# A four-phase kernel: the gated product moves into PSUM, residual work moves between VectorE and GpSimd, and the last normalisation is shared out anew

## The chip, the cores and the metric

The kernel runs on one core of one Trainium2 chip. The metric is the device time of one execution, in microseconds (us). Three executions of the kernel before took 1301.18, 1302.83 and 1308.39 us; the median is 1302.83 us. The names of the engines in the profile are PE (TensorE matmuls), PEld (TensorE weight loads), DVE (VectorE), ACT (ScalarE), POOL (GpSimd) and SP (SyncE).

## The reference, cut to what matters

The input is x of shape (2, 2048, 128). Four blocks follow one another, each as x = x + layernorm(block(layernorm(x))): an RWKV-like time mix with its channel mix, a ternary-weight feed-forward, a state-space block and a mixture of 8 experts of which each token uses 2. The change touches the first and the last.

```python
# the time mix (L0_attn), per batch and channel
xxx = h + (h - x_shifted) * ts                     # h = layernorm of the block's input
k, v, r = xxx @ Wk.T, xxx @ Wv.T, sigmoid(xxx @ Wr.T)
wkv = scan over time: out = (e1 * aa + e2 * vv) / (e1 + e2), with the running maximum bb
x = x + r * wkv                                    # the residual that the change moves
# the mixture of experts (L1_ffn), top 2 of 8
h = silu(x @ w1[e]) * (x @ w3[e])                  # the gated product
out = sum over the 2 experts of  weight_e * (h @ w2[e])
# around it
x = x + (out - mean(out)) / sqrt(var(out) + eps)
```

## The kernel before, in words

Channels lie on the 128 partitions. The 2 x 2048 tokens are cut into NT = 4 tiles of N = 512 tokens for each of B = 2 batches. Each phase is a block with one instruction stream for each engine, written out by hand; engines meet only at semaphores, and a phase ends with a barrier of all engines. Nothing schedules the order: it is that of the code.

**The time mix** (`phase_time_mix`, lines 164 to 600). VectorE does most of it, tile by tile. For tile t and each batch b it runs `sums` (a scan over `fac`, line 520), `normalise` of tile t+1 (lines 471 and 474: `pC` in PSUM times `rstd` in SBUF), `shift_and_mix`, `distances` (line 528), `maxima`, `weigh_values`, `steps`, `ln2_scale` of tile t-1, `clip_steps`, `numerators` (a scan, line 544) and `blend` (lines 552, 556 and 559, each for both batches). `blend` ends with line 562, which copies the last column of two running rows to their first column by a multiplication and maximum over 4 elements. GpSimd then multiplies the blended value by the gate (line 439) and adds the residual (line 441), for batch 0 and then batch 1. `ln2_centre` on TensorE reads that sum, and ScalarE squares it (`ln2_square`). ScalarE's stream is in order: behind the squares of tile t-1 stand the exponentials of tile t, which `weigh_values` (line 539) needs.

**The mixture** (`phase_moe`, line 1857 and on). Routing sorts the token-expert pairs into TILES = 39 tiles of 256 rows, each for one expert. For each tile GpSimd issues two indirect DMAs that gather rows (line 2277) and two that scatter the results (line 2294). The first 8 tiles are gathered ahead; from then on GpSimd's stream is scatter tile i, gather tile i+8. TensorE turns the rows (`x_turn`), VectorE copies them out as 16-bit pairs (`take_x`, line 2504), and two units n of each tile follow: `up` (24 matmuls a tile at lines 2014 to 2016) writes the two products of a unit into the banks `R1` and `R3`; ScalarE takes silu of `R1` (line 2231); VectorE multiplies `R3` by it into `hid` in SBUF (line 2520); ScalarE rounds `hid` to 16 bits (`hid_high`, line 2217); VectorE writes the rest, `hid` less its rounded value (`hid_low_part`, line 2511); `down`, LAG = 3 units later, multiplies both by w2; ScalarE copies the result into one of 4 buffers `y` (line 2223), which GpSimd scatters.

**The end** (same function). The DMA queue of SP reads all results back, in 8 groups of 4 chunks of 128 tokens. For group i VectorE adds the two experts' rows and their sums (`add_up`, line 2535, with the sums in `sums`), and makes `minus`, the negated means (line 2540); ScalarE squares the deviations with their sums (`spread`, line 2245) and forms the inverse root; VectorE multiplies twice over 4 columns (`weigh`, `scale_of`); GpSimd scales the group (line 2307, four instructions of 128x128); TensorE turns it (line 2154); VectorE adds it to X (`add_out`, line 2556); SP stores it. `scaled` and the bank `R1` each have two buffers.

## Time and profile before

| what | value |
|---|---|
| three executions, median | 1302.83 us |
| the profiled execution's own time | 1301.92 us |
| its span in the trace | 1300.1 us |
| time mix, to its barrier | 0 to about 133 us |
| channel mix and feed-forward, state-space block | about 133 to 985 us |
| routing of the mixture | to about 1062 us |
| the 39 tiles of the mixture | about 1062 to 1264 us |
| read back, last normalisation, stores | to the end |

The profiled execution lies between the lowest and the median of the three. The busy time of an engine is the sum of its instructions' spans; matmuls overlap in the records, so a PE that is busy in all of a window need not be at its peak. In a timeline row the bracket is the idle time ahead of the instruction and what ended it; "issue" means that nothing the profile shows was waited for.

### The profile page before, as it was taken

What the parts mean: (1) busy time and instruction counts of PE and PEld (TensorE: products, weight loads), DVE (VectorE), ACT (ScalarE), POOL (GpSimd) and SP (SyncE); (2) the same over time, 40 slices, a digit from 0 to 9 for tenths busy, and PEclk for the clock granted to TensorE, in tenths of its full rate; (3) what the DMA queues carried; (4) which work ended last, traced back from release to release, by engine and by line L of the source; (5) the groups of instructions that cost most, each with busy time, mean ns of one, the idle gap of its engine ahead of it and who ended that gap; (6) DMA issues with size and microseconds to landing.
All of it is one profiled execution on the core that took longest, in us unless ns stands there. A gap on an engine that the chain in (4) does not pass through costs nothing. (4 is left out here: it accounts for less than half of the span.)

```text
span 1300.1 us, 16587 instructions
## 1 busy us (share of the span) xinstructions
PE 1073.6 (83%) x4914; PEld 543.4 (42%) x4914; DVE 985.6 (76%) x1333; ACT 731.6 (56%) x1163; POOL 738.3 (57%) x617
## 2 busy tenths in 40 slices
PE   6655669999999997979898898989797569988853
PEld 2211224444444442433333333434233459977753
DVE  6996776575664546999999999999993587765535
ACT  6773454555645446748575675766563336544434
POOL 0223342151421202899889889897985257777764
PEclk8885799999999997999999999999998569998986
DMA  6000000000000002323232322222220111111225
GB/s 228 1 1 0 0 1 1 1 2 1 0 0 0 1 0 82 102 69 109 71 98 72 100 89 90 74 72 70 70 73 1 65 30 51 49 50 51 49 50 193
DMA packets 32552, 67.07 MB, mean 52 GB/s; under 512 B 5760, under 2 KB 5952, under 8 KB 32256
## 3 DMA queue, kind: packets, MB, share of 16 engines
q1 hardware_dynamic: 27056, 55.16, 13.0%
q0 software_dynamic: 4992, 10.23, 2.9%
q8 instruction: 39, 0.64, 0.2%
q10 hardware_dynamic: 432, 0.76, 0.2%
q14 instruction: 33, 0.27, 0.1%
HBM read 56.57 MB, written 9.57 MB: 51 GB/s over the span
## 5 line engine op out<-in xcount | busy, mean ns | idle before, releaser
L1750 POOL TENSOR_TENSOR prod<-hs,csb 128x1024 f32<-128x1024 f32 x128 | 301.9, 2359 | 139.1 <-DVE hs L1797 138.5
L1797 DVE TENSOR_TENSOR_SCAN hs<-dA,carry,pD 128x512 f32<-128x512 f32 x256 | 313.8, 1267 | 5.2 <-DVE pD L1810 0.8
L1519 PE MATMUL pY<-prod,const 128*128 128x512 f32 x512 | 247.0, 606 | 1.8 <-POOL prod L1750 1.8
L1659 ACT ACTIVATE dA<-dt,negA 128x512 f32<-128x512 f32 x256 | 168.0, 713 | 17.3 <-POOL dt L1719 15.8
L1810 DVE TENSOR_TENSOR pD<-dtu,pD 128x1024 f32<-128x1024 f32 x128 | 155.3, 1214 | 7.5 <-PE pD L1533 7.4
L1519 PEld LDWEIGHTS pY<-prod,const 128*128 128x128 f32 x512 | 97.6, 194 | 119.3 <-issue 114.7
L2277 POOL DMA_INDIRECT g<-moe_rows,source x78 | 83.1, 1065 | 49.7 <-DVE source L2469 26.3
L2520 DVE SCALAR_TENSOR_TENSOR hid<-pR,silu 128x512 f32<-128x512 f32 x78 | 53.9, 691 | 63.1 <-ACT silu L2231 63.1
L1003 ACT ACTIVATE stage<-pR,vec 128x512 f32<-128x512 f32 x64 | 43.9, 687 | 100.2 <-PE pR L703 100.0
L2294 POOL DMA_INDIRECT moe_outs<-y,to x78 | 82.1, 1052 | 24.8 <-issue 22.8
L2014 PE MATMUL pR<-x,moe_hi 128*128 128x256 f16 x312 | 87.3, 280 | 2.2 <-DVE x L2504 2.2
L2015 PE MATMUL pR<-x,moe_hi 128*128 128x256 f16 x312 | 87.5, 280 | 0.0
L2016 PE MATMUL pR<-x,moe_lo 128*128 128x256 f16 x312 | 87.2, 279 | 0.0
L2231 ACT ACTIVATE silu<-pR 128x512 f32<-128x512 f32 x78 | 46.5, 596 | 59.6 <-PE pR L2016 58.7
L1053 POOL TENSOR_TENSOR z_lo<-z,z_hi 128x512 f16<-128x512 f32 x8 | 10.6, 1326 | 106.2 <-DVE z_hi L1140 106.2
L1448 PE MATMUL pQ<-xn,convw 128*128 128x512 f32 x112 | 58.4, 646 | 13.6 <-DVE xn L1780 13.6
L439 POOL TENSOR_TENSOR o<-o,rs 128x512 f32<-128x512 f32 x8 | 14.4, 1800 | 97.2 <-DVE o L559 97.2
L1533 PE MATMUL pD<-split,sel 96*128 96x512 bf16 x128 | 50.1, 392 | 19.3 <-DVE hs L1797 18.9
L1042 POOL TENSOR_TENSOR K_lo<-kstage,K_hi 128x512 f16<-128x512 f32 x24 | 28.8, 1203 | 53.7 <-DVE K_hi L1115 53.7
L2126 PE MATMUL pY<-moe_hi,hid_hi 128*128 x312 | 57.8, 223 | 0.8 <-DVE hid_lo L2511 0.8
L2128 PE MATMUL pY<-moe_hi,hid_lo 128*128 x312 | 57.8, 223 | 0.0
L2127 PE MATMUL pY<-moe_lo,hid_hi 128*128 x312 | 57.7, 223 | 0.0
(423 smaller groups left out, 2574.2 us busy)
## 6 DMA issues: line engine op xcount, KB each, us to landing
csb<-ssm_c SPq DMA_DIRECT2D x128, 256.0 KB, 3.1
raw<-moe_w SPq DMA_DIRECT2D x12, 512.0 KB, 4.9
room<-moe_outs SPq DMA_DIRECT2D x8, 512.0 KB, 8.0
hidw<-hid_w SPq DMA_DIRECT2D x1, 2048.0 KB, 9.9
moe_rows<-xt SPq DMA_DIRECT2D x8, 256.0 KB, 2.0
outT<-X SPq DMA_DIRECT2D x8, 256.0 KB, 2.0
X<-xT SPq DMA_DIRECT2D x3, 512.0 KB, 4.1
g<-moe_rows,source POOLq DMA_INDIRECT x78, 2.8
```

Source lines behind the costliest of these rows:

```text
L1448: last = nc.tensor.matmul(Q[c][:], convw[:, c, k, :], xn[b][:, k:k + N], start=k == 0, stop=k == TAPS - 1)
L1519: last = nc.tensor.matmul(YB[c][:], G.ident, prod[:, slot(b, n), c, :], start=n == 0, stop=n == DST - 1)
L1659: last = nc.scalar.activation(dA[:, slot(b, n), c, :], dt[:, b, c, :], ACT.Exp, scale=negA[:, c, n:n + 1])
L1750: nc.gpsimd.tensor_tensor(prod[:, slot(b, n), :, :], hs[:, slot(b, n), :, :], csb[:, slot(b, n), :, :].to_broadcast([P, CB, N]), ALU.mult)\
L1797: last = nc.vector.tensor_tensor_scan(hs[:, slot(b, n), c, :], dA[:, slot(b, n), c, :], dBu(n, c), carry[:, b, n, c:c + 1], ALU.mult, ALU.add)
L1810: nc.vector.tensor_tensor(DD[:, (n % 2) * CB:(n % 2) * CB + CB, :], dtu[:, b, :, :], bcastB(n).unsqueeze(1).to_broadcast([P, CB, N]), ALU. ...
L2014: nc.tensor.matmul(out, w_hi, x_hi, start=start, stop=False)
L2015: nc.tensor.matmul(out, w_hi, x_lo, start=False, stop=False)
L2016: return nc.tensor.matmul(out, w_lo, x_hi, start=False, stop=stop)
L2126: nc.tensor.matmul(out, hid_hi[:, n % HR, at], w_hi, start=u == 0 and h == 0 and r == 0, stop=False)
L2277: nc.gpsimd.indirect_dma_start(g[:, i % GR, r, :], None, rows, bass.IndirectOffsetOnAxis(ap=source[:, 2 * i + r:2 * i + r + 1], axis=0))\
L2294: nc.gpsimd.indirect_dma_start(outs, bass.IndirectOffsetOnAxis(ap=to[:, 2 * i + r:2 * i + r + 1], axis=0), y[:, i % YR, r, :], None).then_ ...
```

## The change

In the time mix VectorE takes over part of GpSimd's work. In `blend` of tiles 0 to 2 batch 1 goes first, and its gate product and residual sum are done by VectorE; GpSimd does only batch 0's two. In the last tile VectorE does all four. The copy of the carried columns at the end of `blend` is gone; `steps` carries the columns of the sums and numerators with those it carried already, and the last tile has a small copy of its own (`carry_numerators`). `normalise` of tile t+1 stands ahead of `sums` in every tile, and on ScalarE `inverse_roots` ahead of `step_exponentials`.

In the mixture `hid` in SBUF is gone. The product stays in the bank of `R3` from which it was read; `R3` has three banks in place of two, `XG` one in place of two, and the small uses of the second XG bank go to the third of `R3`. `up` of unit n waits for `hid_low` of unit n-3 and for silu of unit n-2, where it waited for the product of unit n-2.

At the end `spread` takes `sums` itself and scales by -128; the factor is taken out again in the logarithm's scale. `minus` is made by GpSimd. GpSimd scales groups 0 to 5; VectorE scales groups 6 and 7 (`scale_up`).

```diff
                 if t + 2 < NT:
                     square(t + 2)
+                    inverse_roots(t + 2)
                 if t + 1 < NT:
                     step_exponentials(t + 1)
-                if t + 2 < NT:
-                    inverse_roots(t + 2)
...
-            for t in range(NT):
-                for b in range(B):
-                    pool.wait_ge(S["shift"], at(t, b))
-                    pool.wait_ge(S["gate"], at(t, b))
-                    nc.gpsimd.tensor_tensor(o[:, b, :], o[:, b, :], rs[:, t % 2, b, :], ALU.mult).then_inc(S["gated"], 1)
-                    pool.wait_ge(S["gated"], at(t, b))
-                    nc.gpsimd.tensor_tensor(XA[:, b, ds(t)], o[:, b, :], xn[:, t % 3, b, :], ALU.add)\
-                      .then_inc(S["added"], 1)
+            for t in range(NT - 1):
+                pool.wait_ge(S["shift"], B * t + 2)
+                pool.wait_ge(S["gate"], at(t, 0))
+                nc.gpsimd.tensor_tensor(o[:, 0, :], o[:, 0, :], rs[:, t % 2, 0, :], ALU.mult).then_inc(S["gated0"], 1)
+                pool.wait_ge(S["gated0"], t + 1)
+                nc.gpsimd.tensor_tensor(XA[:, 0, ds(t)], o[:, 0, :], xn[:, t % 3, 0, :], ALU.add).then_inc(S["added0"], 1)
...
-                nc.vector.tensor_copy(run[:, :, 0:2, 0:1], run[:, :, 0:2, N:N + 1]).then_inc(S["carried"], 1)
+                if t >= 1:
+                    dve.wait_ge(S["logsum"], at(t - 1, B - 1))
+                if t >= 2:
+                    dve.wait_ge(S["shift"], at(t - 2, B - 1))
+                ends = slice(0, min(t, 2) + 2)
+                nc.vector.tensor_copy(run[:, :, ends, 0:1], run[:, :, ends, N:N + 1]).then_inc(S["carried"], 1)
...
+            def carry_numerators(t):
+                dve.wait_ge(S["shift"], at(t, B - 1))
+                nc.vector.tensor_copy(run[:, :, 3:4, 0:1], run[:, :, 3:4, N:N + 1]).then_inc(S["carried"], 1)
+
+            def difference(t, b):
+                dve.wait_ge(S["numer"], at(t, b))
+                if t >= 1:
+                    dve.wait_ge(S[f"added{b}"], t)
+                nc.vector.tensor_tensor(o[:, b, :], V[b][:], run[:, b, 3, 0:N], ALU.subtract).then_inc(S["diff"], 1)
+
+            def weighted(t, b, nth):
+                dve.wait_ge(S["diff"], at(t, B - 1))
+                dve.wait_ge(S["vweight"], at(t, b))
+                nc.vector.tensor_tensor(o[:, b, :], o[:, b, :], wv[:, b, :], ALU.mult).then_inc(S["blend"], 1)
+                dve.wait_ge(S["blend"], B * t + nth)
+                nc.vector.tensor_tensor(o[:, b, :], o[:, b, :], run[:, b, 3, 0:N], ALU.add).then_inc(S["shift"], 1)
+
+            def gated_residual(t, b, nth):
+                dve.wait_ge(S["shift"], B * t + nth)
+                dve.wait_ge(S["gate"], at(t, b))
+                nc.vector.tensor_tensor(o[:, b, :], o[:, b, :], rs[:, t % 2, b, :], ALU.mult).then_inc(S[f"gated{b}"], 1)
+                dve.wait_ge(S[f"gated{b}"], t + 1)
+                nc.vector.tensor_tensor(XA[:, b, ds(t)], o[:, b, :], xn[:, t % 3, b, :], ALU.add)\
+                  .then_inc(S[f"added{b}"], 1)
+
             def blend(t):
                 for b in range(B):
-                    dve.wait_ge(S["numer"], at(t, b))
-                    if t >= 1:
-                        dve.wait_ge(S["added"], at(t - 1, b))
-                    nc.vector.tensor_tensor(o[:, b, :], V[b][:], run[:, b, 3, 0:N], ALU.subtract).then_inc(S["diff"], 1)
-                for b in range(B):
-                    dve.wait_ge(S["diff"], at(t, b))
-                    dve.wait_ge(S["vweight"], at(t, b))
-                    nc.vector.tensor_tensor(o[:, b, :], o[:, b, :], wv[:, b, :], ALU.mult).then_inc(S["blend"], 1)
-                for b in range(B):
-                    dve.wait_ge(S["blend"], at(t, b))
-                    nc.vector.tensor_tensor(o[:, b, :], o[:, b, :], run[:, b, 3, 0:N], ALU.add).then_inc(S["shift"], 1)
-                dve.wait_ge(S["shift"], at(t, B - 1))
-                carry = run[:, :, 2:4, N:N + 1]
-                nc.vector.scalar_tensor_tensor(out=run[:, :, 2:4, 0:1], in0=carry, scalar=1.0, in1=carry, op0=ALU.mult,
-                                               op1=ALU.max).then_inc(S["carried_sums"], 1)
+                    difference(t, b)
+                if t < NT - 1:
+                    weighted(t, 1, 1)
+                    gated_residual(t, 1, 1)
+                    weighted(t, 0, 2)
+                else:
+                    for b in range(B):
+                        weighted(t, b, b + 1)
+                        gated_residual(t, b, b + 1)
...
             for t in range(NT):
-                if t == 0:
+                if t + 1 < NT:
                     normalise(t + 1)
                 sums(t)
-                if t >= 1 and t + 1 < NT:
-                    normalise(t + 1)
                 if t + 1 < NT:
                     shift_and_mix(t + 1)
...
-        hid = sb("hid4", [P, HR, 2 * ROWS])
...
-        total = hid[:, :, :].rearrange("p r (j d) -> p r j d", j=TC)
+        total = sb("total4", [P, 4, TC, P])
...
-        R3 = mem.enter_context(nc.psum_tensor("pR3_4", [P, 2, N], F32))
-        XG = mem.enter_context(nc.psum_tensor("pX4", [P, 2, N], F32))
+        R3 = mem.enter_context(nc.psum_tensor("pR3_4", [P, UPS, N], F32))
+        XG = mem.enter_context(nc.psum_tensor("pX4", [P, N], F32))
...
+        spare_bank = R3[:, UPS - 1, :]
...
             def x_turn(i):
                 pe.wait_ge(S[f"gathered{i % GR}"], 32 * (i // GR + 1))
-                if i >= 2:
-                    pe.wait_ge(S["x_in"], i - 1)
+                if i >= 1:
+                    pe.wait_ge(S["x_in"], i)
...
                 if n >= 2:
-                    pe.wait_ge(S["hidden"], n - 1)
+                    pe.wait_ge(S["silus"], n - 1)
+                if n >= UPS:
+                    pe.wait_ge(S["hid_low"], n - UPS + 1)
                 for h in range(2):
-                    for out, at in ((R1, 0), (R3, FFN)):
+                    for out, at in ((R1[:, u, :], 0), (R3[:, n % UPS, :], FFN)):
...
             for i in range(GROUPS):
-                pe.wait_ge(S["scaledC"], i + 1)
+                if i < MOST:
+                    pe.wait_ge(S["scaledC"], i + 1)
+                else:
+                    pe.wait_ge(S["scaledD"], i - MOST + 1)
...
-                nc.scalar.activation(hid_hi[:, n % HR, :], hid[:, n % HR, :], ACT.Copy).then_inc(S["hid_high"], 1)
+                nc.scalar.activation(hid_hi[:, n % HR, :], R3[:, n % UPS, :], ACT.Copy).then_inc(S["hid_high"], 1)
...
-                act.wait_ge(S["minus"], i + 1)
+                act.wait_ge(S["summed"], i + 1)
                 for j in range(TC):
                     c = i * TC + j
                     last = nc.scalar.activation(xn[:, i % 2, j * P:(j + 1) * P], total[:, i % 4, j, :], ACT.Square,
-                                                bias=minus[:, c:c + 1], accum_out=var[:, c:c + 1])
+                                                bias=sums[:, c:c + 1], scale=-float(P), accum_out=var[:, c:c + 1])
                 last.then_inc(S["squaredC"], 1)
...
+            def negate(i):
+                pool.wait_ge(S["summed"], i + 1)
+                nc.gpsimd.tensor_scalar(minus[:, slab(i)], sums[:, slab(i)], -1.0 / P, None, ALU.mult)\
+                  .then_inc(S["minus"], 1)
+
+            negate(0)
+            for i in range(MOST):
+                negate(i + 1)
+                if i == MOST - 1:
+                    negate(GROUPS - 1)
+                pool.wait_ge(S["minus"], i + 1)
                 pool.wait_ge(S["scale"], i + 1)
...
-                nc.vector.tensor_tensor(hid_lo[:, n % HR, :], hid[:, n % HR, :], hid_hi[:, n % HR, :], ALU.subtract)\
+                nc.vector.tensor_tensor(hid_lo[:, n % HR, :], R3[:, n % UPS, :], hid_hi[:, n % HR, :], ALU.subtract)\
...
                 dve.wait_ge(S["silus"], n + 1)
-                if n >= HR:
-                    dve.wait_ge(S["hid_low"], n - HR + 1)
-                nc.vector.scalar_tensor_tensor(out=hid[:, n % HR, :], in0=R3[:, u, :], scalar=1.0 / WS,
+                nc.vector.scalar_tensor_tensor(out=R3[:, n % UPS, :], in0=R3[:, n % UPS, :], scalar=1.0 / WS,
                                                in1=silu[:, u, :], op0=ALU.mult, op1=ALU.mult).then_inc(S["hidden"], 1)
...
-                dve.wait_ge(S["summed"], i + 1)
-                nc.vector.tensor_scalar(minus[:, slab(i)], sums[:, slab(i)], -1.0 / P, None, ALU.mult)\
-                  .then_inc(S["minus"], 1)
...
+            def scale_up(i):
+                dve.wait_ge(S["minus"], i + 1)
+                dve.wait_ge(S["scale"], i + 1)
+                dve.wait_ge(S["turnedC"], i - 1)
+                for j in range(TC):
+                    c = i * TC + j
+                    last = nc.vector.tensor_scalar(scaled[:, i % 2, j * P:(j + 1) * P], total[:, i % 4, j, :],
+                                                   minus[:, c:c + 1], scale[:, c:c + 1], ALU.add, ALU.mult)
+                last.then_inc(S["scaledD"], 1)
...
-                if i >= 4:
+                if i - 2 == MOST:
+                    add_out(i - 4)
+                if MOST <= i - 2 < GROUPS:
+                    scale_up(i - 2)
+                if i >= 4 and i - 2 != MOST:
```

VectorE's stream in the time mix, from the last instruction of `difference` in tile 0 to the start of tile 1; `o` is the blended value, `rs` the gate, `run` the running rows, `pC`, `pV` and `pK` are PSUM banks. Before:

```order
L552 TENSOR_TENSOR o<-pV_1,run 128x512
L556 TENSOR_TENSOR o<-o,wv 128x512 x2
L559 TENSOR_TENSOR o<-o,run 128x512 x2
L562 SCALAR_TENSOR_TENSOR run<-run 128x2x2
L520 SCALAR_TENSOR_TENSOR run<-fac,run 128x512 x2
L471 TENSOR_TENSOR xn<-pC_0,rstd 128x512
L474 SCALAR_TENSOR_TENSOR run<-pC_0,vec,rstd 128x512
L471 TENSOR_TENSOR xn<-pC_1,rstd 128x512
L474 SCALAR_TENSOR_TENSOR run<-pC_1,vec,rstd 128x512
L484 TENSOR_SCALAR mix<-run,vec 128x512 x2
L488 SCALAR_TENSOR_TENSOR mix<-run,small,mix 128x512 x2
```

and now:

```order
L559 TENSOR_TENSOR o<-pV_1,run 128x512
L564 TENSOR_TENSOR o<-o,wv 128x512
L566 TENSOR_TENSOR o<-o,run 128x512
L571 TENSOR_TENSOR o<-o,rs 128x512
L573 TENSOR_TENSOR XA<-o,xn 128x512
L564 TENSOR_TENSOR o<-o,wv 128x512
L566 TENSOR_TENSOR o<-o,run 128x512
L468 TENSOR_TENSOR xn<-pC_0,rstd 128x512
L471 SCALAR_TENSOR_TENSOR run<-pC_0,vec,rstd 128x512
L468 TENSOR_TENSOR xn<-pC_1,rstd 128x512
L471 SCALAR_TENSOR_TENSOR run<-pC_1,vec,rstd 128x512
L522 SCALAR_TENSOR_TENSOR run<-fac,run 128x512 x2
```

The four instructions of `normalise` moved ahead of the scans over `fac`, the small instruction of line 562 is gone, and two more instructions on batch 1 stand in the middle of `blend`.

GpSimd's stream at the end of the mixture; `moe_outs` is the scatter's target, `sq` the scaled group. Before:

```order
L2277 DMA g<-moe_rows,source 128x256 x2
L2294 DMA moe_outs<-y,to 18176x128 x2
L2277 DMA g<-moe_rows,source 128x256 x2
L2294 DMA moe_outs<-y,to 18176x128 x16
L2307 ISA
L2307 TENSOR_SCALAR sq<-hid,minus,scale 128x128 x32
```

and now:

```order
L2323 DMA moe_outs<-y,to 18176x128 x16
L2332 ISA
L2332 TENSOR_SCALAR minus<-sums 128x4 x2
L2346 TENSOR_SCALAR sq<-total,minus,scale 128x128 x4
L2332 TENSOR_SCALAR minus<-sums 128x4
L2346 TENSOR_SCALAR sq<-total,minus,scale 128x128 x4
L2332 TENSOR_SCALAR minus<-sums 128x4
```

The negations stand between the scalings, one group ahead of them; 24 scalings are left of 32.

VectorE's stream at the end, from the last groups' products over 4 columns on. Before:

```order
L2545 TENSOR_TENSOR var<-var,squared_share 128x4
L2550 TENSOR_TENSOR scale<-var,share 128x4
L2556 TENSOR_TENSOR X<-X,pR_4 128x512
L2545 TENSOR_TENSOR var<-var,squared_share 128x4
L2550 TENSOR_TENSOR scale<-var,share 128x4
L2556 TENSOR_TENSOR X<-X,pR_4 128x512
L2550 TENSOR_TENSOR scale<-var,share 128x4
L2556 TENSOR_TENSOR X<-X,pR_4 128x512 x3
```

and now:

```order
L2579 TENSOR_TENSOR var<-var,squared_share 128x4
L2584 TENSOR_TENSOR scale<-var,share 128x4
L2600 TENSOR_TENSOR X<-X,pR_4 128x512
L2579 TENSOR_TENSOR var<-var,squared_share 128x4
L2584 TENSOR_TENSOR scale<-var,share 128x4
L2600 TENSOR_TENSOR X<-X,pR_4 128x512
L2593 TENSOR_SCALAR sq<-total,minus,scale 128x128 x4
L2584 TENSOR_TENSOR scale<-var,share 128x4
L2593 TENSOR_SCALAR sq<-total,minus,scale 128x128 x4
L2600 TENSOR_TENSOR X<-X,pR_4 128x512 x3
```

`scale_up` of group 6 follows `add_out` of group 4, and that of group 7 stands ahead of `add_out` of group 5.

## Rows read from the trace of the kernel before

**Rows 1.** Page, section 4: the chain that ended last, by engine.

```profile
POOL 8%; issue 4%; DVE 3%; PE 3%; DMA 2%; ACT 1%; SPq 0%; POOLq 0%; DVEq 0%; ACTq 0%
```

**Rows 2.** Windows: stretch, length, PE, PEld, DVE, ACT, POOL busy; clock, DMA.

```profile
1130.00:1262.00 132.00, 106.33 (x1229) 93.54 (x1226) 75.12 (x117) 61.13 (x120) 102.27 (x98) 0.95 0.20 51
```

**Rows 3.** Groups by line, POOL, 1074.5 to 1265; columns as section 5.

```profile
L2294 POOL DMA_INDIRECT moe_outs<-y,to x78 | 82.1, 1052 | 24.8 <-issue 22.8 <-ACT y L2223 2.0
L2277 POOL DMA_INDIRECT g<-moe_rows,source x62 | 65.1, 1050 | 18.9 <-issue 17.7 <-PE pX L2093 0.9 <-ACT y L2223 0.3
```

**Rows 4.** Timeline, POOL and DVE: start us, length us, what, idle before.

```profile
1074.87 1.05 POOL L2294 DMA_INDIRECT moe_outs<-y,to  x1 [1.37 <-ACT y L2223]
1097.16 0.68 DVE L2511 TENSOR_TENSOR hid_lo<-hid,hid_hi 128x512 f16<-128x512 f32 x1
1097.41 1.29 POOL L2294 DMA_INDIRECT moe_outs<-y,to  x1 [0.30 <-issue]
1098.53 0.69 DVE L2520 SCALAR_TENSOR_TENSOR hid<-pR,silu 128x512 f32<-128x512 f32 x1 [0.69 <-ACT silu L2231]
1099.00 0.99 POOL L2277 DMA_INDIRECT g<-moe_rows,source  x1 [0.30 <-issue]
1100.30 0.96 POOL L2277 DMA_INDIRECT g<-moe_rows,source  x1 [0.30 <-issue]
1103.20 0.98 POOL L2294 DMA_INDIRECT moe_outs<-y,to  x1 [0.30 <-issue]
1107.34 1.00 POOL L2294 DMA_INDIRECT moe_outs<-y,to  x1 [0.30 <-issue]
```

**Rows 5.** Timeline, PE, DVE and ACT, in the tiles.

```profile
1065.06 0.42 PE L2015 MATMUL pR<-x,moe_hi 128*128 128x256 f16 x1
1069.03 0.28 PE L2014 MATMUL pR<-x,moe_hi 128*128 128x256 f16 x1
1068.80 0.73 DVE L2511 TENSOR_TENSOR hid_lo<-hid,hid_hi 128x512 f16<-128x512 f32 x1
1073.69 0.38 ACT L2223 ACTIVATE y<-pY 128x256 f32<-128x256 f32 x1
1085.35 0.60 ACT L2231 ACTIVATE silu<-pR 128x512 f32<-128x512 f32 x1 [0.86 <-PE pR L2016]
1089.53 0.60 ACT L2231 ACTIVATE silu<-pR 128x512 f32<-128x512 f32 x1 [0.86 <-PE pR L2016]
```

**Rows 6.** Timeline of DVE and POOL in the time mix.

```profile
26.71 2.45 DVE L520 TENSOR_TENSOR_SCAN run<-fac,run 128x512 f32<-128x512 f32 x2
44.97 1.29 DVE L559 TENSOR_TENSOR o<-o,run 128x512 f32<-128x512 f32 x2
46.29 1.11 DVE L562 SCALAR_TENSOR_TENSOR run<-run 128x4 f32<-128x4 f32 x1
47.51 4.46 DVE L520 TENSOR_TENSOR_SCAN run<-fac,run 128x512 f32<-128x512 f32 x2
50.97 2.07 POOL L441 TENSOR_TENSOR XA<-o,xn 128x512 f32<-128x512 f32 x1
51.89 0.66 DVE L471 TENSOR_TENSOR xn<-pC,rstd 128x512 f32<-128x512 f32 x1
74.12 4.45 DVE L520 TENSOR_TENSOR_SCAN run<-fac,run 128x512 f32<-128x512 f32 x2
```

**Rows 7.** Timeline of DVE and POOL in its last tile.

```profile
110.00 0.69 DVE L539 TENSOR_TENSOR bv<-pV,fac 128x512 f32<-128x512 f32 x1 [1.24 <-ACT fac L384]
123.88 1.28 POOL L441 TENSOR_TENSOR XA<-o,xn 128x512 f32<-128x512 f32 x1
```

**Rows 8.** A small POOL copy by source, then the timeline at the end.

```profile
L1743 POOL COPY carry<-hs x128: 175/185/280, 511.6 to 989.2; 128x2 f32<-128x2 f32 x128
1287.20 1.73 POOL L2307 TENSOR_SCALAR sq<-hid,minus,scale 128x128 f32<-128x128 f32 x4 [0.25 <-DVE scale L2550]
1294.07 0.69 DVE L2556 TENSOR_TENSOR X<-X,pR 128x512 f32<-128x512 f32 x1 [0.35 <-PE pR L2154]
```

More of the change, by code:

```diff
@@ L594, in _ @@
                     clip_steps(t + 1)
+                else:
+                    carry_numerators(t - 1)
                 numerators(t)
@@ L2025, in variance @@
                     pe.wait_ge(S["logs"], late(i))
-                nc.tensor.matmul(XG[:, 1, :], G.ones, sq[:, i % 2, :], start=True, stop=True)\
+                nc.tensor.matmul(spare_bank, G.ones, sq[:, i % 2, :], start=True, stop=True)\
                   .then_inc(S["variance"], 1)
@@ L2064, in _ @@
             flat_so_far = so_far[:, :, :].rearrange("p e c -> p (e c)")
-            nc.tensor.matmul(XG[:, 1, 0:E * CHUNKS], later[:, :], flat, start=True, stop=False)
+            nc.tensor.matmul(spare_bank[:, 0:E * CHUNKS], later[:, :], flat, start=True, stop=False)
             pe.wait_ge(S["so_far"], 1)
@@ L2068, in _ @@
               .then_inc(S["counted"], 1)
-            nc.tensor.matmul(XG[:, 1, 0:E * CHUNKS], ones16[:, :], flat_so_far, start=False, stop=True)\
+            nc.tensor.matmul(spare_bank[:, 0:E * CHUNKS], ones16[:, :], flat_so_far, start=False, stop=True)\
               .then_inc(S["ranked"], 1)
@@ L2299, in _ @@
                     gather(i + AHEAD)
-            for i in range(GROUPS):
+            def negate(i):
[8 more added lines that the diff above has]
+                pool.wait_ge(S["minus"], i + 1)
                 pool.wait_ge(S["scale"], i + 1)
```

40 lines of the change are left out of this document (22 added, 18 removed).

## The prediction

> **What bounds the kernel now.** I read the chain of waits first. Its largest engine is POOL [rows 1], and in order of time those pieces are one stretch: the 39 tiles of the mixture. The time by window, from 1130 to 1262 us, shows why: 98 instructions of POOL are busy 102.3 of 132 us, and PE 106.3 [rows 2]. That alone decides nothing, so the groups of POOL come next. From the first scatter to the last, 78 scatters and 62 gathers take 147.2 us, and POOL is idle for 43.7 us, of which 40.5 are "issue", the 0.30 us ahead of each DMA [rows 3, 4]. Less than 4 us are a wait for anybody. So POOL issues without a pause for 190 us, 1.05 + 0.30 us a DMA, four to a tile: 5.40 us a tile. TensorE needs less. While it had gathered tiles in store, silu of the same parity recurred after 1089.53 - 1085.35 = 4.18 us [rows 5]. The tiles last as long as POOL's 140 instructions.
>
> Then the timeline of POOL beside that of DVE. The same scatter takes 0.98 or 1.00 us at 1103.20 and 1107.34 and 1.29 us at 1097.41; gathers take 0.99 and 0.96 us [rows 4]. The long one began 0.25 us into `hid_low_part`, which ran from 1097.16 to 1097.84. The gather at 1099.00 began inside the product of line 2520 and took its 0.99 us [rows 4]. Going through all 140, 35 begin inside line 2511 with more than 0.18 us of it left, and they average 1.26 us; the other 105 average 0.98 us. So the instruction with two inputs in SBUF holds up the start of a DMA on POOL, and the one with an input in PSUM doesn't.
>
> The time mix is bound by DVE, which has no gap there except at its first tile and its last. The same thing is seen: two scans over `fac` take 2.45 us alone and 4.46 us while POOL multiplies and adds, and `normalise`, one input in PSUM, takes 0.66 us beside a POOL instruction [rows 6]. Line 562 touches 4 elements and takes 1.11 us, to the end of POOL's instruction.
>
> **The tiles of the mixture.** The product now stays in PSUM, so `hid_low_part` reads PSUM and SBUF. No VectorE instruction of the tiles has two SBUF inputs any more. With clean lengths the DMAs would be 78 x 0.99 + 62 x 0.975 = 137.7 us in place of 147.2: 9.5 us less. The gaps stay.
>
> The Trainium skill bears on this from both sides. Its page SBUF — State Buffer, section "Who interferes with whom", says that a VectorE instruction with two SBUF inputs contends with a GpSimd instruction that reads SBUF, and that one with at most one does not, outside the 2-port modes; rows 4 and 6 agree. In brackets the same section infers that `tensor_tensor` does not hold up descriptor generation, because that needs the write side; by that the 9.5 us would be 0. The rows at 1097.41 and 1099.00 speak for the first reading (here each DMA also reads its row numbers from SBUF).
>
> What is paid: `up` of unit n waits for `hid_low` of unit n-3. At the start `up` of unit 3 began at 1069.03, and `hid_low` of unit 0 ends at 1068.80 + 0.73 = 1069.53 [rows 5]. It starts 0.5 us later, with it `y` of tile 0 (1073.69) and the first scatter (1074.87). `up` of unit 4 has `down` in front of it and isn't late again. In the steady state `hid_low` of unit n-3 is VectorE's next instruction after the product of n-2 (one copy may lie between), and TensorE has two `down` and one `up` in that time; a stall of a few tenths is covered by 5.13 - 4.18 = 0.95 us a tile. The single `XG` bank adds no wait, since `up` of the same tile already waits for that copy. That VectorE and ScalarE now use PSUM for the product: silu, which reads PSUM, takes 0.60 us, and line 2520, which reads it, 0.69 [rows 4, 5]; neither engine is near full. Term: -9.5 + 0.5 = **-9.0 us**; bounds -11 (the last waits gone as well) and 0.
>
> **The time mix.** Per tile change, between tiles 0 and 1, and 1 and 2:
> - The scans come after `normalise` (4 instructions, 2.5 us in which POOL does its two of 1.28 us each, row 1.28 in [rows 7]). So they cost 2.45, not 4.46 us: -2.0; 0.25 us of POOL's second is left over: +0.25.
> - Line 562 goes: from 46.26, the end of line 559, to the scans at 47.51: -1.2 [rows 6].
> - `blend` was six instructions in two interleaved rows, each 0.60 us after the other (two take 1.29, one 0.69) [rows 6]: 5 x 0.60 + 0.69 = 3.7 us. Now it is eight, of which six wait for the one ahead: 0.60 + 0.69 + 6 x 0.71 = 5.55: +1.85.
>
> That is -1.1 us, twice. Between tiles 2 and 3 there is no `normalise`, and the scans still meet POOL: -1.2 + 1.85 = +0.65. Tile 3 starts 1.55 us sooner.
>
> In tile 3 `weigh_values` waits for ScalarE's exponentials (110.00, after 1.24 us of idle) [rows 7], which stand behind the square that needs POOL's residual. POOL has only two instructions now but starts 1.8 us later against this tile's scans, and gives way to a scan each time: residual done 5.0 us into the tile, two centrings at 1.9 us each on a slow TensorE, the square, then the exponential: 10.5 us into the tile, where it was 9.3. That takes back 1.2, the copy of the carry 0.15. At the end VectorE does everything itself: 1.26 + 8 x 0.71 = 6.9 us from the end of the scan to the last residual, where POOL ended 8.6 us after it (123.88 + 1.28 = 125.16 [rows 7], the scan at 116.54): -1.7. `inverse_roots` ahead of the exponentials on ScalarE costs 2.2 us a batch there; by my sum both are ready 1 us or more before VectorE asks. Sum -1.55 + 1.2 + 0.15 - 1.7 = **-1.9 us**; bounds -5 (TensorE fast in the last tile) and +3 (roots or exponentials late by 1 to 1.5 us a tile).
>
> **The end.** POOL scales a group in 1.73 us alone and about 2.0 beside VectorE [rows 8]. With one small instruction more (0.19, as its copy of 2 elements [rows 8]) and a gap it takes about 2.35 us a group. VectorE loses `minus` (0.26 us a group) and ScalarE starts a bit sooner, but group 5 leaves POOL about when it did or up to 1 us later, since POOL is then the slowest. After it come one turn, `scale_up` of group 7 (0.6 us), `add_out` of 5 and the turn of 7. Before, POOL had two more groups there, 3.4 us. I get the last `add_out`, now at 1294.07 [rows 8], 0.4 to 1.0 us sooner within this part: **-0.7 us**; bounds -2.5 and +1.
>
> **Sum.** -9.0 - 1.9 - 0.7 = -11.6. On the profiled execution, 1301.92 us (span 1300.1 and 1.8 around it), that is 1290.3. The median of the runs is 0.9 us above it; I take a third of that: 1290.6 us.
>
> **Rivals.**
> 1. *The long DMAs are not VectorE's doing*, or the product in PSUM doesn't free POOL. For it: short DMAs too lie beside line 2511, when it starts after them. Against: 35 of 35 that start inside it are long. Then the tiles give +0.5: 1301.9 - 1.9 - 0.7 + 0.5 = 1299.8 us. Chance 8 in 100. The bracket of the Trainium skill's page SBUF — State Buffer, cited above, would lead here.
> 2. *Only part of it comes.* POOL gives its 9.5 us, but the time mix comes out at its bad bound (roots late in three tiles, +3) and the end at +1: 1301.9 - 9.0 + 3 + 1 = 1297. Or half of the DMAs stay long for another reason: 1295. Together 9 in 100.
> 3. *TensorE becomes the bound, slower than before.* Place: the tiles. `up` waits on the longer chain, TensorE idles, and its granted clock, 0.95 in the mean of rows 2, falls. At the lower level a matmul of 256 columns holds its place 0.21 us (1065.06, length 0.42) in place of 0.11 [rows 5], and a tile costs about 8.1 us in place of 5.13. Three such tiles in a row eat the gain, six make it 1301.9 - 11.6 + 18 = 1308. It decides once a tile needs over 5.4 us on TensorE. Against: POOL's faster pace leaves TensorE less idle, and the slack is 0.95 us. 5 in 100.
> 4. *More comes*: TensorE fast in the last tile of the time mix, the end at -2.5: 1301.9 - 9.5 - 5 - 2.5 = 1285. 8 in 100.
>
> The forecast, 1290.6 us with 1287 to 1294 as its own range, has 70 in 100. From 1285 to 1297 about 8 in 10 are held. A measurement of this kernel tells about 0.5%, 6.5 us, from no change: faster than 1296.3 is 86 in 100, within 0.5% 9, slower 5.
>
> **What would show it.** The mean of POOL's gathers and scatters at 0.98 us and none above 1.1 while tiles run; the first scatter half a microsecond later against the first `take_x`; line 562's place empty, the scans of tiles 1 and 2 at 1.25 us each and those of tile 3 slow; VectorE waiting in tile 3 for about 3 us; the last eight instructions of `blend` 5.7 us long. It is wrong if DMAs of 1.3 us remain, if PE or ACT are what POOL waits for in the tiles, or if VectorE waits for `rstd` ahead of `normalise`.

## The result, and the profile after

| | before | after |
|---|---|---|
| median of the executions | 1302.62 us (4) | 1286.39 us (4) |
| lowest and highest | 1301.18, 1308.39 | 1284.78, 1288.61 |
| profiled execution, span | 1300.1 | 1284.6 |

By the medians that is 16.2 us faster, where the forecast said 12. The ratio is 0.9863, 95% interval 0.9832 to 0.9894, which makes 17.8 us. Two further comparisons, below, gave 0.9855 [0.9831, 0.9879] and 0.9885 [0.9869, 0.9901]. The mechanism was there as forecast; the gain at the tile changes of the time mix was put too small, and one piece of the gain stood in no term.

The tiles of the mixture first. The groups of POOL after, from the first scatter to the last, answer to [rows 3] (line numbers are 29 higher):

```profile
L2323 POOL DMA_INDIRECT moe_outs<-y,to x78 | 77.1, 988 | 24.4 <-issue 21.9 <-ACT y L2252 2.5
L2306 POOL DMA_INDIRECT g<-moe_rows,source x62 | 60.5, 975 | 18.9 <-issue 18.3 <-ACT y L2252 0.6
```

The 140 DMAs take 137.6 us in place of 147.2, with the same counts and almost the same gaps. The window from the first scatter to the last (length; PE, PEld, DVE, ACT, POOL busy; clock, DMA), before and then after:

```profile
1074.87:1264.35 189.48, 161.46 (x1917) 145.06 (x1915) 116.64 (x183) 94.30 (x186) 147.14 (x140) 0.96 0.19 50
1071.17:1251.09 179.92, 159.02 (x1917) 140.74 (x1915) 116.29 (x183) 94.73 (x186) 137.56 (x140) 0.99 0.20 53
```

TensorE's granted clock rose from 0.96 to 0.99, so rival 3 is out. The timeline of VectorE and POOL holds the twin of the long scatter in [rows 4]: it too begins 0.25 us into `hid_low_part`, whose first input is now `pR` in PSUM, and takes 0.98 us where it took 1.29.

```profile
1092.84 0.68 DVE L2550 TENSOR_TENSOR hid_lo<-pR,hid_hi 128x512 f16<-128x512 f32 x1
1093.09 0.98 POOL L2323 DMA_INDIRECT moe_outs<-y,to  x1 [0.30 <-issue]
```

Of the 140, 29 begin with more than 0.18 us of `hid_low_part` left, and none of all 140 is longer than 1.00 us. Before, 31 were over 1.1 us.

The price at the start of the tiles shows too. The first `take_x`, silu of unit 3 and the first scatter, before ([rows 4] has the scatter, at 1074.87) and then after:

```profile
1062.02 0.69 DVE L2504 CAST x<-pX 128x512 f16<-128x512 f32 x1
1070.55 0.60 ACT L2231 ACTIVATE silu<-pR 128x512 f32<-128x512 f32 x1 [0.56 <-PE pR L2016]
```

```profile
1057.61 0.68 DVE L2543 CAST x<-pX 128x512 f16<-128x512 f32 x1
1066.85 0.60 ACT L2260 ACTIVATE silu<-pR 128x512 f32<-128x512 f32 x1 [1.29 <-PE pR L2040]
1071.17 1.00 POOL L2323 DMA_INDIRECT moe_outs<-y,to  x1 [0.95 <-ACT y L2252]
```

The granted clock is 0.87 in both stretches, and silu of unit 2 comes 6.86 us after the first `take_x` in both. Silu of unit 3 comes 9.24 us after it in place of 8.53, and the first scatter 13.56 in place of 12.85: 0.7 us later, where the forecast had 0.5.

The time mix after, VectorE and POOL, answers to [rows 6, 7]. First the change from tile 0 to tile 1, then that from 2 to 3, then the last tile:

```profile
49.48 0.74 DVE L471 SCALAR_TENSOR_TENSOR run<-pC,vec,rstd 128x512 f32<-128x512 f32 x1
51.39 2.54 DVE L522 TENSOR_TENSOR_SCAN run<-fac,run 128x512 f32<-128x512 f32 x2
...
99.23 3.42 DVE L522 TENSOR_TENSOR_SCAN run<-fac,run 128x512 f32<-128x512 f32 x2
99.39 2.18 POOL L437 TENSOR_TENSOR o<-o,rs 128x512 f32<-128x512 f32 x1 [22.55 <-DVE o L566]
101.65 2.06 POOL L439 TENSOR_TENSOR XA<-o,xn 128x512 f32<-128x512 f32 x1
102.58 2.29 DVE L530 TENSOR_TENSOR lns<-lns,xx 128x512 f32<-128x512 f32 x2
...
109.02 0.69 DVE L541 TENSOR_TENSOR bv<-pV,fac 128x512 f32<-128x512 f32 x1 [2.81 <-ACT fac L384]
122.00 0.69 DVE L573 TENSOR_TENSOR XA<-o,xn 128x512 f32<-128x512 f32 x1
```

Where `normalise` stands between, two scans take 2.54 us. Where it doesn't, they take 3.42, but not the 4.45 of before, since POOL now has two instructions there and not four. VectorE's wait in the last tile grew from 1.24 to 2.81 us, as forecast.

At the end VectorE now scales two groups, and its last addition stands at 1280.30:

```profile
1277.28 1.12 DVE L2593 TENSOR_SCALAR sq<-total,minus,scale 128x128 f32<-128x128 f32 x4
1278.31 1.28 DVE L2600 TENSOR_TENSOR X<-X,pR 128x512 f32<-128x512 f32 x2
1280.30 0.69 DVE L2600 TENSOR_TENSOR X<-X,pR 128x512 f32<-128x512 f32 x1 [0.72 <-PE pR L2183]
```

From there to the end of the span are 3.6 us; in the kernel before they were 5.4. That piece stood in no term of the sum. What it is can be read from the instructions that close the program, which the page doesn't count as work. First the kernel before, then the changed one (length in ns, start in us):

```profile
L1880 POOLq DRAIN  x1: 7632/7632/7632, 1291.2 to 1291.2; - x1
L1880 PEldq DRAIN  x1: 1188/1188/1188, 1292.9 to 1292.9; - x1
L1880 SPq DRAIN  x1: 7/7/7, 1297.0 to 1297.0; - x1
L1880 SPq EVENT_SEMAPHORE  x1: 17/17/17, 1299.0 to 1299.0; - x1
```

```profile
L1904 POOLq DRAIN  x1: 8027/8027/8027, 1273.4 to 1273.4; - x1
L1904 SPq DRAIN  x1: 7/7/7, 1283.3 to 1283.3; - x1
L1904 SPq EVENT_SEMAPHORE  x1: 17/17/17, 1283.4 to 1283.4; - x1
```

POOL's last scaling ended at 1292.82 before and its drain at 1298.79, 6.0 us later. SP had the last store landed by 1297.0 and waited 2.0 us more. After, POOL's last instruction ends at 1275.48 and its drain at 1281.4, ahead of SP's drain behind the last store at 1283.3. From the later of the two to the end of the span are 1.3 us in both. The drain ends 6.0 us after POOL's last instruction in all 13 profiles here. The trace names PE as what SP waited for, but PE's drain ended at 1294.1; the release is an inference, and here it points at the wrong engine.

### The profile page after: what moved, and what is told of

It is laid out like the page before. It is cut to its first block and busy times, and to the rows that moved or that the text cites. A ratio compares the mean times of both kernels' runs of the same rounds, so it can differ in the third digit from the quotient of the medians.

```text
span 1284.6 us, 16559 instructions
## 1 busy us (share of the span) xinstructions
PE 1072.4 (83%) x4914; PEld 537.9 (42%) x4914; DVE 985.0 (77%) x1340; ACT 732.1 (57%) x1163; POOL 709.8 (55%) x607
## 5 line engine op out<-in xcount | busy, mean ns | idle before, releaser
L2306 POOL DMA_INDIRECT g<-moe_rows,source x78 | 78.5, 1007 | 50.0 <-DVE source L2508 26.5
L2557 DVE SCALAR_TENSOR_TENSOR pR<-pR,silu 128x512 f32<-128x512 f32 x78 | 54.6, 700 | 57.7 <-ACT silu L2260 57.7
L2323 POOL DMA_INDIRECT moe_outs<-y,to x78 | 77.1, 988 | 24.4 <-issue 21.9
L2038 PE MATMUL pR<-x,moe_hi 128*128 128x256 f16 x312 | 85.8, 275 | 1.9 <-DVE x L2543 1.2
L2039 PE MATMUL pR<-x,moe_hi 128*128 128x256 f16 x312 | 85.7, 275 | 0.0
L1556 PE MATMUL pD<-split,sel 96*128 96x512 bf16 x128 | 50.1, 391 | 19.3 <-DVE hs L1820 18.9
L437 POOL TENSOR_TENSOR o<-o,rs 128x512 f32<-128x512 f32 x3 | 4.7, 1575 | 93.7 <-DVE o L566 93.7
```

The source lines that it names most:

```text
L2038: nc.tensor.matmul(out, w_hi, x_hi, start=start, stop=False)
L2039: nc.tensor.matmul(out, w_hi, x_lo, start=False, stop=False)
L2306: nc.gpsimd.indirect_dma_start(g[:, i % GR, r, :], None, rows, bass.IndirectOffsetOnAxis(ap=source[:, 2 * i + r:2 * i + r + 1], axis=0))\
L2323: nc.gpsimd.indirect_dma_start(outs, bass.IndirectOffsetOnAxis(ap=to[:, 2 * i + r:2 * i + r + 1], axis=0), y[:, i % YR, r, :], None).then_ ...
```

## The stages in every profile

The landmarks are the first scan over K; the copy that ends the time mix; the first scan of the state-space block and the start of its last pair of scans; the first gather; the first scatter's start and the last one's end; the first `add_up`; the end of the last `add_out`; the end of the span. Lengths between them in us, one profile each:

| stage | before | end_only | tiles_only | mix_only | after | after_again | after_third |
|---|---|---|---|---|---|---|---|
| to the first scan | 19.0 | 21.3 | 21.5 | 21.5 | 19.9 | 19.8 | 21.5 |
| **time mix** | 113.3 | 113.9 | 113.8 | 110.7 | 110.3 | 110.3 | 110.6 |
| to the state-space block | 374.4 | 376.0 | 376.0 | 376.1 | 375.5 | 375.5 | 376.1 |
| state-space block | 477.7 | 477.6 | 481.0 | 480.7 | 477.7 | 477.6 | 480.7 |
| to the first gather | 66.5 | 64.2 | 66.2 | 65.6 | 64.2 | 65.9 | 66.3 |
| to the first scatter | 24.0 | 23.0 | 23.8 | 23.4 | 23.6 | 23.7 | 24.8 |
| **tiles** | 189.5 | 189.1 | 179.6 | 192.1 | 179.9 | 179.6 | 179.8 |
| to the first add_up | 6.0 | 6.2 | 6.1 | 6.0 | 6.1 | 6.4 | 6.0 |
| **end** | 24.4 | 23.8 | 24.5 | 25.6 | 23.8 | 23.6 | 23.3 |
| **closing piece** | 5.4 | 3.6 | 5.4 | 4.6 | 3.6 | 3.6 | 3.6 |

The four bold stages go with the change; the others take values that don't follow it. Two bold stages also vary where their part of the kernel is unchanged: the time mix took 113.3 to 113.9 us without its part, and the tiles 189.1 to 192.1 us without theirs. In the first difference of profiles (15.5 us) they happened to cancel nearly: +0.9, +1.1, 0, -2.3, -0.4, +0.1. The bold stages give 3.0 + 9.6 + 0.6 + 1.8 = 15.0 us. The 0.7 us at the start of the tiles lies in a stage that isn't bold; less that, the change made 14.3 us of the difference.

## Experiments

**Each part alone** (end_only, tiles_only, mix_only), and the changed kernel again. The edits are the three parts of the diff: the lines of `phase_time_mix`; those of the tiles with the banks; those from `MOST` on.

> The kernel before with the part of the change at the end alone. Theory: first add_up to last add_out 23.8 us in place of 24.4, the kernel 0.6 us faster, within 0.5% all the same. Rival (the end part also shortens what follows the last store, 3.6 us in place of 5.4): 2.4 us faster. If that last piece is chance, it shows 5.4 or 3.6 in kernels without this part too.

> The kernel before with the part of the change in the tiles of the mixture alone (product in PSUM, one bank for the turned x, three for the unit products, the variance and rank in the third). Theory (VectorE's instruction with two SBUF inputs held up the start of POOL's DMAs): every one of the 140 DMAs 0.95 to 1.05 us long, first scatter to last 180 us in place of 189.5, the kernel 9 to 10 us faster. Rival (the other banks make the routing quicker as well, 2.3 us sooner at the first gather): 12 us faster, with no wait of over 1 us for the rows' store before the gathers. Rival (the landing of the rows' store varies by chance): the first gather stands where it did, or moves by up to 3 us in kernels whose change lies elsewhere too.

> The kernel before with the part of the change in the time mix alone. Theory: the time mix ends 2 to 3 us sooner, counted from the first scan over K, and about 1.2 us of it is given back by TensorE's clock until 300 us: the kernel 1 to 3 us faster; the tiles' DMAs as before, a quarter of them 1.26 us long, 189.5 us from first scatter to last. Rival (part given back is chance): 2 to 3 us faster. Rival (what was gained in the routing comes from the time mix's shift): first gather 3.3 us sooner than before.

> The changed kernel once more, in five rounds: ratio 0.987 to 0.989, so 14.5 to 17 us faster. If the two pieces that no part of the change touches (2.3 us in the routing before the first gather, 1.75 us after the last store) are chance, this profile has at least one of them otherwise, and the ratio lies nearer 0.990; if they belong to the change, both are there again.

| kernel | ratio, 95% | us by the ratio | by the bold stages of its part |
|---|---|---|---|
| tiles_only | 0.9942 [0.9925, 0.9960] | -7.6 | -9.9 |
| mix_only | 0.9974 [0.9951, 0.9996] | -3.4 | -2.6 |
| end_only | 0.9990 [0.9972, 1.0007] | -1.3 | -2.3 |
| after_again | 0.9855 [0.9831, 0.9879] | -18.9 | -15.4 |

The tiles and the time mix are each a stage of their own. The theory of mix_only had 1.2 us given back up to the state-space block. That stage is 1.6 to 1.7 us longer than before in mix_only, but also in tiles_only and end_only, which leave the time mix alone, so it isn't the change's doing. The 2.3 us that the first gather came sooner are not the banks' doing: tiles_only has the banks and not the gain, end_only the gain and not the banks. The wait behind it is for the rows' store to land. Of the kernel before, and after:

```profile
1021.17 0.60 ACT L2183 ACTIVATE xt<-pY 128x512 f16<-128x512 f32 x1 [3.17 <-DMA moe_rows<-xt]
```

```profile
1017.61 0.60 ACT L2212 ACTIVATE xt<-pY 128x512 f16<-128x512 f32 x1 [0.61 <-DMA moe_rows<-xt]
```

The closing piece of 3.6 us is in end_only too, so it belongs to the part at the end: my theory had 0.6 us for that part, the rival 2.4, and the rival was right. In mix_only POOL's DMAs were over 1.1 us 37 times in place of 31, and the tiles took 192.1 us: how many of them meet the VectorE instruction depends on how the two streams fall, so this cost isn't a constant either.

By the ratios the parts gave 12 us alone and 19 together. The stages, and the next comparison, speak for chance.

**The changed kernel once more, and without the part at the end:**

> The changed kernel a third time. By the stages that repeat in every profile (time mix 3.2, tiles 9.5, end 0.7, closing piece 1.75) it is 15.2 us faster, ratio 0.988. If the higher sum of the first two comparisons (0.9863 and 0.9855) is what the stages outside the change happened to be in those runs, the ratio lies at 0.987 to 0.990 here and some runs are above 1290 us; rival (the changed kernel's runs are always in the quicker kind of those stages): all runs within 1284 to 1289 us again and the ratio below 0.987.

> The changed kernel without the part at the end. Theory: the end 24.4 in place of 23.8 us and the piece after the last add_out 5.4 in place of 3.6 us, so 2.4 us slower than the changed kernel: ratio to before 0.9885 to 0.990 if the changed kernel has 0.987 in this call. Rival (the three parts help each other beyond their stages: alone they gave 7.5, 3.4 and 1.3 us, together 18.9): ratio 0.991 or more and a stage other than the end that is longer than in the changed kernel.

after_third: 0.9885 [0.9869, 0.9901], executions of 1288.0 to 1294.6 us; its profile has the longer start, state-space block and routing. The theory's 0.988 holds, and the "help" of the parts for each other doesn't come again. no_end: 0.9890 [0.9871, 0.9909], median 1291.93 us against 1290.48; by its stages the end is 24.06 in place of 23.25 us and the closing piece 5.37 in place of 3.62, together 2.6 us. The intervals of the two ratios overlap; the stages tell them apart, the time of the whole doesn't.

**Is it the second SBUF input?** (two_sbuf, one_sbuf, copy_sbuf; one execution each, so only their stages are compared.) One more VectorE instruction per unit, in three forms, its output unused. Each of the three carried an edit in the time mix as well.

```diff
+            def extra_work(n):
+                dve.wait_ge(S["hid_high"], n + 1)
+                ...
+                two = G.const[:, 0:2, :].rearrange("p a c -> p (a c)")
+                nc.vector.tensor_tensor(extra[:, n % 2, :], two, two, ALU.subtract)...     # two_sbuf
+                nc.vector.tensor_tensor(extra[:, n % 2, :], R3[:, n % UPS, 0:ROWS], two, ALU.subtract)...  # one_sbuf
+                nc.vector.tensor_copy(extra[:, n % 2, :], two)...                          # copy_sbuf
...
+                    extra_work(n - 1)
                     hid_low_part(n - 1)
```

The edits in the time mix: two_sbuf puts `sums` ahead of `normalise` again for tiles 1 and 2; one_sbuf gives POOL the gating of the last tile's two batches again; copy_sbuf puts `step_exponentials` ahead of `inverse_roots` again.

> The changed kernel with one more VectorE instruction per unit ahead of hid_low_part, both inputs in SBUF, 128x256, its output not used; and in the time mix the scans ahead of normalise again for tiles 1 and 2. Theory for the tiles (two SBUF inputs on VectorE hold up the start of a DMA on POOL): those DMAs that begin inside the extra instruction are long, by up to 0.4 us each; about one in six would be, so the tiles take 3 to 7 us longer than 179.8 us from first scatter to last. Rival (VectorE being busier, or the later hid_low, is what counts): as long as with the kernel that has the input in PSUM. Time mix: the two tiles get 1.2 to 2 us longer each, its length from the first scan over K goes from 110.3 to 113 or 114 us. Rival (the order is worth nothing beside the removed copy and what waits for the exponentials): under 111 us.

> The changed kernel with the same extra VectorE instruction, but its first input in PSUM; and in the time mix the last tile's gating and residual of both batches on POOL again. Theory for the tiles: all 140 DMAs stay at 0.95 to 1.05 us, first scatter to last 179.5 to 181 us. Rival (a busier VectorE or the later hid_low counts): 183 us or more. Time mix: the last four instructions of VectorE, 2.8 us, go and POOL's four of 1.28 us come behind it, so its length goes from 110.3 to about 112 us.

> The changed kernel with an extra copy on VectorE per unit, one input in SBUF, float32 128x256 to float16; and in the time mix the step exponentials ahead of the inverse roots on ScalarE, as in the kernel before. Theory for the tiles (it is the second SBUF input): 179.5 to 181 us from first scatter to last, no DMA over 1.1 us. Rival (any SBUF read of VectorE, or a copy's faster mode, holds POOL up too): several DMAs at 1.1 to 1.4 us and 182 us or more. Time mix: the roots come 1.2 us later and normalise of tile 2, which now stands first, waits for them: 110.3 goes to 111 to 114 us; if the roots were never late, it stays.

| | after | two_sbuf | one_sbuf | copy_sbuf |
|---|---|---|---|---|
| tiles, us | 179.6 to 179.9 | 183.25 | 180.06 | 179.73 |
| the 140 DMAs, us | 137.3 to 137.6 | 140.9 | 137.7 | 137.4 |
| DMAs over 1.1 us | 0 | 12 | 0 | 0 |
| DMAs over 1.03 us | 0 | 26 | 0 | 0 |
| time mix, us | 110.2 to 110.6 | 113.7 | 112.1 | 110.7 |

The groups of POOL in the tiles, two_sbuf and then one_sbuf; the gaps are equal, the means not:

```profile
L2326 POOL DMA_INDIRECT moe_outs<-y,to x78 | 79.0, 1012 | 24.9 <-issue 22.6 <-ACT y L2255 2.3
L2309 POOL DMA_INDIRECT g<-moe_rows,source x62 | 61.9, 999 | 18.9 <-issue 18.3 <-ACT y L2255 0.3 <-PE pX L2120 0.3
```

```profile
L2330 POOL DMA_INDIRECT moe_outs<-y,to x78 | 77.2, 989 | 24.9 <-issue 21.9 <-ACT y L2259 2.9
L2313 POOL DMA_INDIRECT g<-moe_rows,source x62 | 60.6, 977 | 18.9 <-issue 18.0 <-ACT y L2259 0.9
```

And one held DMA of two_sbuf, which begins 0.09 us into the extra instruction:

```profile
1093.23 0.41 DVE L2561 TENSOR_TENSOR extra<-const 128x256 f16<-128x256 f32 x1
1093.32 1.20 POOL L2326 DMA_INDIRECT moe_outs<-y,to  x1 [0.30 <-issue]
```

The same instruction with one input in PSUM costs nothing, though 30 DMAs begin inside it, 16 of them with more than 0.18 us of it left. So it is the second SBUF input, not a busier VectorE or a later `hid_low`. The excess is what is left of the VectorE instruction when the DMA begins, less about 0.1 us: 0.32 left, 0.22 more; in [rows 4] 0.43 left, 0.31 more. A DMA that begins together with the VectorE instruction isn't held: one in the kernel before began 0.02 us into `hid_low_part`, with 0.72 us of it left, and took 0.99 us.

The copy settles little. It takes 0.28 us, 19 DMAs begin inside it, and none with more than 0.16 us of it left; by the same reckoning a copy that does hold POOL up would have shown 0.06 us at the most. The DMA with 0.16 us left took 1.03 us, the longest of the 140, which is about that. The rival of copy_sbuf, that any SBUF read or a copy's faster mode holds POOL up, is refuted for a read with one SBUF input by one_sbuf and by `hid_low_part` in the changed kernel; for the copy's mode it stays open. The Trainium skill, page SBUF — State Buffer, section "Who interferes with whom", says that two SBUF inputs contend with a GpSimd instruction that reads SBUF; this holds here for the issue of an indirect DMA. Its bracket, that `tensor_tensor` doesn't hold up descriptor generation, doesn't hold for these DMAs: `two - two` is a `tensor_tensor`, and it holds them up by as much as 0.22 us. They also read their row numbers from SBUF; a DMA issued by POOL that reads none wasn't tried.

In the time mix the order of `normalise` and the scans is worth 3.0 us: the changes to tiles 1 and 2, counted from the start of `numerators` to that of `distances`, take 15.85 and 17.10 us in place of 14.98 each. The forecast had twice 1.75 (-2.0 and +0.25 a tile), and that the sum comes near it is chance. At the first change only 0.9 us come back, because POOL has two instructions there to meet the scans and not four. At the second it is 2.1 us, but 0.7 us of it is a wait for exponentials that neither kernel had there:

```profile
77.53 3.86 DVE L522 TENSOR_TENSOR_SCAN run<-fac,run 128x512 f32<-128x512 f32 x2 [0.72 <-ACT fac L379]
```

POOL's gating in the last tile costs 1.7 us, as the forecast had it: from the first `difference` to the last residual 8.67 us in place of 6.95. ScalarE's order is worth nothing that can be told: the three tile changes take 14.98, 14.98 and 11.13 us in copy_sbuf and in the changed kernel alike, so the roots were never late.

**What closes the program** (pool_late, one execution). A small instruction of POOL behind the last turn; and in the time mix's last tile, ScalarE's decay exponentials and value weights ahead of the second norm.

```diff
+            pool.wait_ge(S["turnedC"], GROUPS)
+            nc.gpsimd.tensor_scalar(late_one[:, :], sums[:, 0:4], -1.0 / P, None, ALU.mult)
```

> The changed kernel with one small instruction more on POOL at the very end, behind the last turn, its output not used; and in the time mix's last tile ScalarE's decay exponentials and value weights ahead of the second norm's square and root, VectorE's second norm of tile 2 behind the differences. Theory for the end (the program ends 6.0 us after POOL's last instruction, if the last store has not landed later): the piece after the last add_out grows from 3.6 to about 7.1 us. Rival (TensorE's last 16 matmuls in one row made that piece longer in the kernel before): it stays at 3.6 us. Time mix: VectorE's wait of 2.8 us ahead of weigh_values shrinks to under 1 us and the time mix ends 1 to 2.5 us sooner, 108 to 109.3 us; rival (the second norm's chain on TensorE then ends last): 110 us or more.

The closing piece is 6.89 us in place of 3.6. POOL's extra instruction ends at 1287.32 and the drain at 1293.3, 6.0 us later once more; the rival would have left it at 3.6.

```profile
1287.10 0.22 POOL L2357 TENSOR_SCALAR late_one<-sums 128x4 f32<-128x4 f32 x1 [4.87 <-PE pR L2190]
```

```profile
L1910 POOLq DRAIN  x1: 6226/6226/6226, 1287.1 to 1287.1; - x1
```

The edit in the time mix failed: 113.2 in place of 110.3 us. VectorE's wait ahead of `weigh_values` did shrink to 0.45 us, but the value weights need another table of ScalarE, and behind them each logarithm and each exponential loaded its own again, 1.28 us a time:

```profile
112.44 1.28 ACT L367 ACT_TABLE_LOAD   x1
113.73 0.69 ACT L367 ACTIVATE lnv<-pR,small 128x512 f32<-128x512 f32 x1
114.44 1.28 ACT L372 ACT_TABLE_LOAD   x1
115.73 0.63 ACT L372 ACTIVATE rstd<-lnv 128x512 f32<-128x512 f32 x1
116.38 1.28 ACT L367 ACT_TABLE_LOAD   x1
116.39 0.75 DVE L597 SCALAR_TENSOR_TENSOR G<-pC,vec,rstd 128x512 f32<-128x512 f32 x1 [3.05 <-ACT rstd L372]
```

**A better version** (weights_first): the same idea, with the table that holds both functions loaded once, ahead of the second norm, and VectorE's second norm between the two batches of its blend; at the end three groups on VectorE.

```diff
                 exponentials(t, S["argD"], S["decays"])
-                if t >= 1:
+                if 1 <= t < NT - 1:
                     ln2_inverse_root(t - 1)
+                if t == NT - 1:
+                    ln2_square(t - 1)
                 value_weights(t)
...
                 act.preload_act_table_set("natural_log_exp_and_others")
+                if t == NT - 1:
+                    ln2_inverse_root(t - 1)
...
                         gated_residual(t, b, b + 1)
+                        if b == 0:
+                            ln2_scale(t - 1)
...
-    MOST = GROUPS - 2
+    MOST = GROUPS - 3
```

> The changed kernel with two more edits. In the time mix's last tile ScalarE does the decay exponentials, the second norm's squares and the value weights, and only then the logarithms and roots of the second norm, so that the table is changed once in each direction (the kernel pool_late had changed it five times there, 1.28 us each), and VectorE scales the second norm of tile 2 between the two batches of its blend. At the end VectorE scales three groups in place of two. Theory: VectorE's wait ahead of weigh_values falls from 2.8 to 0.5 us, the last residual comes 3 us sooner, the time mix lasts 107 to 108 us in place of 110.3; the end, first add_up to last add_out, 23.0 to 23.8 us in place of 23.8; the kernel 2.5 to 3.5 us faster than the changed one. Rival (TensorE's slow clock and the second norm's chain of the last tile set the end): time mix 109.5 us or more and no gain. Rival (VectorE becomes the bound of the end): 24.5 us there.

The ratio is 0.9859 [0.9843, 0.9875], median 1287.22 us, beside 0.9885 and 1290.48 for the changed kernel in the same comparison: 3.4 us less by the ratios, though the two intervals overlap a little. The time mix takes 106.9 us, 3.3 to 3.7 less than in the three profiles of the changed kernel, and that stage carries the result. The end isn't shorter (24.0 us, where the changed kernel had 23.3 to 23.8), so the third group on VectorE gave nothing.

## Why the prediction fell short, step by step

| step | forecast | measured |
|---|---|---|
| DMAs of the tiles | -9.5 | -9.6, and as much to 0.3 us in every profile with this part |
| first scatter later by `up` of unit 3 | +0.5 | +0.7, counted from the first `take_x` |
| between tiles 0 and 1, 1 and 2 | 2 x -1.1 | 2 x -1.4 |
| **between tiles 2 and 3** | **+0.65** | **-0.55** |
| last tile, exponentials later | +1.2 | +1.55 |
| carry copy and what is around it | +0.15 | +0.26 |
| end of the blend | -1.7 | -1.75, then +0.3 in the second norm, which varies by more where nothing was changed |
| end, to the last `add_out` | -0.7 | -0.6 |
| **from there to the end of the program** | **none** | **-1.8** |
| sum | -11.6 | -14.3 |

Two steps failed. The first is "Between tiles 2 and 3 there is no `normalise`, and the scans still meet POOL". They do, but they meet two of its instructions and not four: from the scans' start to the next VectorE instruction it is 3.35 us where it was 4.4. I had carried the whole 4.46 over. The steps between the other tiles were 0.3 us too dear each, because what follows the blend began before its last instruction had ended (5.41 us from the blend's start, not 5.55) and the scans needed 2.46 us, not 2.7.

The second is in "The end". The sum was made to the last `add_out`, as if the end of the program followed it at a fixed distance. It follows the later of two things by 1.3 us: the landing of the last store, and a moment 6.0 us after POOL's last instruction. Before the change POOL decided; taking the last two groups from it moved that bound away by more than it moved the last addition. The last instructions of the queues in the trace of before would have shown it: POOL's drain is 7.6 us long there, the others 1.2 us or less.

The two steps together are 1.2 + 0.6 + 1.8 = 3.6 us of gain that the sum had not. The other terms, each off by 0.4 us or less, give back 0.9 of them. Whether a median of whole executions then falls inside the range of 1287 to 1294 is in part luck: the three comparisons gave 1286.39, 1285.45 and 1290.48 us.

What was right: the cause of the long DMAs, though of the 35 that began inside the instruction 34 were long and not all 35; that neither TensorE nor ScalarE took the bound over; the wait of 2.8 us in the last tile ("about 3"); the 5.7 us of the last eight instructions (117.04 to 122.69). Of the rivals, 1 is refuted by the short DMAs and by two_sbuf against one_sbuf, 2 by the roots, which were never late, and by an end that was no longer than before, and 3 by the window's clock. Rival 4 named the right size for the wrong reasons: neither a fast TensorE in the last tile nor the end at -2.5 as it was meant.

What stays open: the measured medians lie 13.8 to 18.6 us under those of before, around the 14.3 of the steps above. Stages outside the change take one of a few lengths: the state-space block 477.6 to 481.0, the start 18.6 to 21.7 us. At the start the first matmuls show it. Four of them in the changed kernel, and in tiles_only:

```profile
4.95 1.98 PE L244 MATMUL pC<-X,const 128*128 128x512 f32 x4
```

```profile
5.14 2.79 PE L244 MATMUL pC<-X,const 128*128 128x512 f32 x4
```

Why an execution gets the one or the other wasn't tried, nor why the rows' store lands later in some.

## What to carry to other kernels

Where POOL issues DMAs back to back and is the bound, look which VectorE instructions have both inputs in SBUF; moving one input to PSUM took 9.6 us from 140 indirect DMAs here. Count the end of a program from the last instruction of every engine, not from the last useful result: POOL's counted for 6.0 us. When whole executions scatter by more than the effect, compare the lengths of the stages in the profiles: with the change in them, the time mix and the tiles repeated within 0.4 us.

## What was not expected of the hardware

POOL's closing drain ended 6.0 us after its last instruction (1292.82 to 1298.8 in the kernel before, 1275.48 to 1281.4 after, 1287.32 to 1293.3 in pool_late), whether POOL had worked up to it or had been idle for 4.9 us in front of it. A VectorE instruction over 4 elements with two SBUF inputs took 1.11 us, to the end of POOL's instruction [rows 6]; the small copy in `steps`, over as many elements, with one input and with POOL idle, takes 0.17 us in the same kernel. Which of the two differences counts wasn't tried for so small an instruction. Value weights ahead of the logarithms gave ScalarE six table loads of 1.28 us in the last tile; with an explicit load of the table that holds both functions, ahead of the first logarithm, there were two.
